# Dispatched experts: transposes at unit 0, a combine over three tiles, groups of 4, 9 and 3 sequences

## What is computed

```python
gate_probs = jax.nn.softmax(x @ Wg + bg, axis=-1)
_, top_idx = jax.lax.top_k(gate_probs, 2)
expert_mask = jax.nn.one_hot(top_idx, 8).sum(-2)
selected = gate_probs * expert_mask
selected = selected / (selected.sum(-1, keepdims=True) + 1e-08)
h = jax.nn.gelu(jnp.einsum('bsf,efh->bseh', x, W1) + b1)
expert_out = jnp.einsum('bseh,ehf->bsef', h, W2) + b2[None, None]
y = jnp.einsum('bsef,bse->bsf', expert_out, selected)
x = _layernorm(x + y, axis=-1)
```

## Time and profile before

| | us |
|---|---|
| median of 3 runs | 3257.44 |
| lowest, highest | 3252.2, 3268.81 |
| the profiled execution | 3267.32 |
| its span | 3265.6 |
| PE busy in it | 2630.8 (81%) |
| DVE busy | 2177.9 (67%) |
| ACT busy | 1415.1 (43%) |
| POOL busy | 1183.2 (36%) |
| stage of the change, from about 2692 to the end | 573 |

### The profile page before, as it was taken

The page is one execution under the profiler, slowest core; times in us unless marked ns, Lnnn a source line. Parts: engine busy times, 40 slices in busy tenths (PEclk is TensorE's granted clock), DMA queues, the critical chain, the costliest instruction groups (busy, mean ns, idle before and its releaser), DMA issues. The chain is left out here.

```text
span 3265.6 us, 51537 instructions
## 1 busy us (share of the span) xinstructions
PE 2630.8 (81%) x17479; PEld 2007.1 (61%) x17479; DVE 2177.9 (67%) x5628; ACT 1415.1 (43%) x2412; POOL 1183.2 (36%) x2298
## 2 busy tenths in 40 slices
PE   1445873999999999858888579999999975888972
PEld 1423662777777777546666467777777754666651
DVE  5733764777777777368888656676767636567684
ACT  0001320555555555412121136666666642776751
POOL 3210111344444434322222124444544444761165
PEclk9997995899999999879999879999999985999996
DMA  2144001222322213021110022212221207776662
GB/s 28 32 142 120 22 10 30 41 39 33 46 35 35 45 29 44 12 100 49 56 56 16 10 35 41 41 29 31 40 36 24 41 2 259 226 248 211 221 208 69
DMA packets 198657, 228.02 MB, mean 70 GB/s; under 512 B 48621, under 2 KB 148814, under 8 KB 190478
## 3 DMA queue, kind: packets, MB, share of 16 engines
q1 hardware_dynamic: 188302, 207.69, 26.4%
q0 software_dynamic: 8192, 16.79, 1.6%
q10 hardware_dynamic: 2048, 2.10, 0.2%
HBM read 132.55 MB, written 58.10 MB: 58 GB/s over the span
## 5 line engine op out<-in xcount | busy, mean ns | idle before, releaser
L1394 PE MATMUL banks<-Kb,Qb 96*128 96x128 f32 (+3 forms) x2048 | 600.0, 348 | 58.7 <-issue 27.1
L1406 PE MATMUL banks<-Qb,Kb 98*128 98x512 f32 (+3 forms) x2048 | 603.4, 356 | 4.8 <-ACT mla_prob L1297 1.0
L1101 DVE TENSOR_REDUCE mha_nm<-banks 128x1 f32<-128x384 f32 (+3 forms) x704 | 421.7, 639 | 189.3 <-PE banks L1398 175.9
L1101 DVE TENSOR_REDUCE mla_nm<-banks 128x1 f32<-128x384 f32 (+3 forms) x704 | 419.6, 637 | 157.2 <-PE banks L1398 143.8
L1297 ACT ACTIVATE mla_prob<-banks 128x512 f32<-128x512 f32 x640 | 376.6, 598 | 306.0 <-PE banks L1406 297.8
L1394 PEld LDWEIGHTS banks<-Kb,Qb 96*128 96x128 f32 x2048 | 364.2, 195 | 216.6 <-issue 157.4
L1297 ACT ACTIVATE mha_prob<-banks 128x512 f32<-128x512 f32 x640 | 376.0, 599 | 276.9 <-PE banks L1406 264.1
L1216 POOL TENSOR_SCALAR_AFFINE_SELECT mla_prob<-mla_prob 128x256 f32<-128x256 f32 (+1 forms) x640 | 239.1, 382 | 397.4 <-PE banks L1394 373.5
L1406 PEld LDWEIGHTS banks<-Qb,Kb 98*128 98x128 f32 x2048 | 335.3, 193 | 45.4 <-issue 6.0
L1216 POOL TENSOR_SCALAR_AFFINE_SELECT mha_prob<-mha_prob 128x256 f32<-128x256 f32 (+1 forms) x640 | 227.0, 363 | 357.3 <-PE banks L1394 331.2
L2174 DVE TENSOR_TENSOR moe_hl<-moe_h,moe_hh 128x512 fp32r<-128x512 f32 x212 | 146.6, 692 | 123.1 <-ACT moe_h L2278 118.2
(11 more groups left out here) (434 smaller groups left out, 5438.3 us busy)
## 6 DMA issues: line engine op xcount, KB each, us to landing
moe_wt<-expert_rows SPq DMA_DIRECT2D x53, 1024.0 KB, 5.1
conv_tz<-conv_kernel SPq DMA_DIRECT2D x16, 1024.0 KB, 6.8
moe_xg<-slots SPq DMA_DIRECT2D x53, 256.0 KB, 4.5
results<-moe_yt SPq DMA_DIRECT2D x53, 256.0 KB
Kb<-mla_kh SPq DMA_DIRECT2D x32, 256.0 KB, 5.0
Qb<-mla_qh SPq DMA_DIRECT2D x128, 64.0 KB
Kb<-mha_kh SPq DMA_DIRECT2D x32, 256.0 KB, 5.6
Qb<-mha_qh SPq DMA_DIRECT2D x128, 64.0 KB
```

The source lines that it names most:

```text
L1101: dve.tensor_reduce(nm[:, g % 2, h:h + heads, j], ps[:, bank1(g, k), 0:heads * w].rearrange("p (h k) -> p h k", h=heads), axis=AX.X, op=AL ...
L1394: one = pe.matmul(ps[:, bank, x * w:(x + 1) * w], Qb[0:MROW, u, g, h + x, j * P:(j + 1) * P], Kb[0:MROW, u, g, 0:w], start=(x == 0), stop= ...
L1406: last = pe.matmul(ps[:, S2 + k % 2, at:at + w], Kb[0:MROW + 2, u, grp, kb * P:(kb + 1) * P], Qb[0:MROW + 2, u, grp, h, kb * P:L], start=T ...
```

## The change

`TURN` becomes 0, 0, 1: the next tile's transposes follow unit 0, DVE's difference unit 1. `back` moves to unit 1, `keep` to unit 2. The combine is cut: at tile g DVE does the first half after unit 0 and the second half after unit 2, at tile g+1 the moments after unit 0, and at tile g+2 ACT normalises after unit 2 with four activations (scale and bias from a column each). POOL's root gets two more small operations, for the bias. The groups are 4, 9 and 3 sequences: 15, 25 and 13 tiles, still 53. The combines of group 0 stand at tiles 20, 22, 24, 25, of group 1 at 45, 47, 49, 50; the condition g + 2 < 53 puts the other five of group 1 with the three of group 2 into `LATE`, eight sequences. Experts 4 to 7 are prepared by DVE after `gates(1)` and by ACT after all sources and `power(1)`. The counts of group 0 come one sequence earlier.

```diff
-        GROUPS = ((0, 4), (4, 8), (12, 4))
+        GROUPS = ((0, 4), (4, 9), (13, 3))
-        TURN = dict(pe=1, act=1, dve=2)
-        EVAC, BACK, KEEP = 3, 0, 1
-        COUNT, POWER = GROUPS[0][1] + 4, GROUPS[0][1] + 4
+        TURN = dict(pe=0, act=0, dve=1)
+        EVAC, BACK, KEEP = 3, 1, 2
+        NORM = dict(dve=0, act=2)
+        COUNT, POWER = GROUPS[0][1] + 3, GROUPS[0][1] + 3
+        ORDER = [(q, j) for q, (_, n) in enumerate(GROUPS) for j in range(n)]
+        for i, (q, j) in enumerate(ORDER):
+            g = FIRST[q + 1] + 5 + (8 * j + 4) // 5 if q + 1 < len(GROUPS) else ALL
+            if g + 2 < ALL:
+                COMBINE[g] = i
+            else:
+                LATE.append(i)
...
+                def first_half(i):
                     dve.wait_ge(gathered[p], c.next(gathered[p], 2 * BLK * 16))
+                    if i >= 2:
+                        dve.wait_ge(out_ready, c.next(out_ready))
...
-                def norm(q, j):
-                    n, p = GROUPS[q][0] + j, j % 2
-                    dve.wait_ge(rstd_ready, c.next(rstd_ready))
...
-                    if q == 0:
+                    gates(q)
+                    if q == 1:
                         for e in range(RAWS, E1):
                             weights(e)
-                    gates(q)
...
                         if m == 0 and g in COMBINE:
-                            combine(*COMBINE[g])
-                        if m == EVAC and g in COMBINE:
-                            norm(*COMBINE[g])
+                            first_half(COMBINE[g])
+                        if m == 2 and g in COMBINE:
+                            second_half(COMBINE[g])
+                        if m == NORM["dve"] and g - 1 in COMBINE:
+                            moments(COMBINE[g - 1])
...
                 def root(p):
                     pool.wait_ge(mv_ready, c.next(mv_ready))
-                    pool_rstd(pool, c, pdone, mv[:, p, :, :], var[:, p, :], mhalf, rstd[:, p, :]).then_inc(rstd_ready, 1)
+                    pool.tensor_scalar(neg[:, p, :], mv[:, p, :, 0], -1.0, 0.0, ALU.mult, ALU.add)
+                    chain(pool, c, pdone, pool_rstd(pool, c, pdone, mv[:, p, :, :], var[:, p, :], mhalf, rstd[:, p, :]))
+                    pool.tensor_tensor(nmr[:, p, :], neg[:, p, :], rstd[:, p, :], ALU.mult).then_inc(rstd_ready, 1)
...
+                for i, (q, j) in enumerate(ORDER):
+                    early = j == 0 and i and i - 1 not in LATE
+                    if early:
+                        root((i - 1) % 2)
+                    if j == 0:
+                        pool.wait_ge(res_ready, c.next(res_ready))
+                    if i >= 2:
+                        pool.wait_ge(g_free, c.next(g_free))
...
+                    if i and not early:
+                        root((i - 1) % 2)
+                root((NB - 1) % 2)
...
+                power(1)
+                for e in range(RAWS, E1):
+                    weights(e)
+                power(2)
...
+                def norm(i):
+                    act.wait_ge(rstd_ready, c.next(rstd_ready))
+                    for b in range(BLK):
+                        last = act.activation(X[:, n, b, :], r[:, p, b, :], ACT.Identity,
+                                              bias=nmr[:, p, b:b + 1], scale=rstd[:, p, b:b + 1])
+                    last.then_inc(out_ready, 1)
```

More of the change, by code:

```diff
@@ L1998, in _ @@
                     load_x(g)
-                for g in range(ALL + 2):
+                for g in range(ALL + 3):
                     if g + XBUFS + 1 < ALL:
                         load_x(g + XBUFS + 1)
-                    if g >= 2:
+                    if 2 <= g < ALL + 2:
                         store_tile(g - 2)
@@ L2007, in _ @@
                         load_w(g + WBUFS - 1)
[L2008 to L2012, removed]
+                    if g - 3 in COMBINE:
+                        store_out(COMBINE[g - 3])
+                for i in LATE:
+                    store_out(i)
                 sp.wait_ge(stored, NB * 16)
@@ L2136, in combine, with moments @@
                     dve.sem_inc(g_free, 1)
+                def moments(i):
+                    p = i % 2
                     block_stats(dve, c, done, r[:, p, :, :], st, mv[:, p, :, :]).then_inc(mv_ready, 1)
-                def norm(q, j):
-                    n, p = GROUPS[q][0] + j, j % 2
-                    dve.wait_ge(rstd_ready, c.next(rstd_ready))
-                    for b in range(BLK):
-                        last = dve.tensor_scalar(X[:, n, b, :], r[:, p, b, :], mv[:, p, b, 0:1],
-                                                 rstd[:, p, b:b + 1], ALU.subtract, ALU.mult)
-                    link(last)
-                    dve.sem_inc(out_ready, 1)
                 def evacuate(g):
@@ L2187, in _ @@
                 keep(ALL - 1)
-                for i, (q, j) in enumerate(LATE):
-                    combine(q, j)
-                    if i:
-                        norm(*LATE[i - 1])
-                norm(*LATE[-1])
+                for i in LATE:
+                    first_half(i)
+                    second_half(i)
+                    moments(i)
             @block.gpsimd
@@ L2216, in _ @@
                                     X[:, first + j, b, :], None).then_inc(scattered[q], 16)
-                taken = 0
-                for q, (first, n) in enumerate(GROUPS):
-                    pool.wait_ge(res_ready, c.next(res_ready))
-                    for j in range(n):
-                        if taken >= 2:
-                            pool.wait_ge(g_free, c.next(g_free))
-                        taken += 1
-                        for b in range(BLK):
-                            for a in range(2):
-                                t = BLK * j + b
-                                pool.indirect_dma_start(
-                                    gb[:, j % 2, a, b, :], None, res_d[q],
-                                    bass.IndirectOffsetOnAxis(back_slot[:, q, a, t:t + 1], 0)).then_inc(gathered[j % 2], 16)
-                        if j:
-                            root((j - 1) % 2)
-                    root((n - 1) % 2)
+                for i, (q, j) in enumerate(ORDER):
[7 more added lines that the diff above has]
+                    for b in range(BLK):
+                        for a in range(2):
+                            t = BLK * j + b
+                            pool.indirect_dma_start(
+                                gb[:, i % 2, a, b, :], None, res_d[q],
+                                bass.IndirectOffsetOnAxis(back_slot[:, q, a, t:t + 1], 0)).then_inc(gathered[i % 2], 16)
+                    if i and not early:
+                        root((i - 1) % 2)
+                root((NB - 1) % 2)
             @block.scalar
@@ L2280, in _ @@
                             high_x((g + 1) % 2)
+                        if m == NORM["act"] and g - 2 in COMBINE:
+                            norm(COMBINE[g - 2])
+                for i in LATE:
+                    norm(i)
             @block.tensor
```

23 lines of the change are left out of this document (11 added, 12 removed).

## The result

The changed kernel takes 3246.2 us (median of 17 runs), the kernel before 3264.5 in as many runs beside it: a ratio of 0.9944, 95% interval 0.9931 to 0.9956. It is faster by 18.3 us, by little more than half of the 31.7 us of the sum. The 3246.2 us lie inside the range of 3211 to 3250, but outside the forecast's own 3215 to 3240; the kernel before was 7 us slower here than the 3257.4 from which the forecast counted.

The account below looks back on a forecast made before the run. PE bounds the loop, waiting each tile for DVE's difference of its input; scatter bounds before it, POOL after. 13.6 − 31.9 − 13.4 = −31.7 us, so 3257.4 becomes 3226 us, range 3211 to 3250.

Parts of the forecast that it names:

- Piece 1: Start of the stage to tile 0's first matmul: late expert weights delay it by 13.6 us, bounds +7.6 and +18.
- S: The start of tile 0, its first matmul: 2776.8 before, forecast at 2790.4.
- Rival A: At the start, tile 0's rows pass the weights or the weights' writes are quicker: 3213 to 3220 us; chance 0.12.
- The plain tile: In the loop, a tile without a combine takes 6.45 us instead of 7.39, as PE's wait goes.
- B: DVE or ACT lag in the loop, plain tiles take 6.9 us or combines stay dear: 3245 us; chance 0.20.
- C: PE waits at each unit's second product instead, tiles stay at 7.39 us: 3274 us, just slower; chance 0.07.
- D: Each normalisation reloads ACT's table, four times in piece 2: +10 to +20 us, 3241; chance 0.03.
- I count 4 us for group 0: Extra time of group 0's combines in the loop: 4 us, bounds 1 and 9.
- I cost it at nothing: In the loop, DMA share rises from 0.76 to 0.87; queues hold four tiles of weights ahead, so no cost.
- Piece 3: From group 1's first gather to the end, POOL's chain: 162 us instead of 175.4, −13.4.
- Rival E: Only half of 16 combines are spread and the tail dominates: piece 3 10 us longer, 3236 to 3246; chance 0.10.
- piece 2: From tile 0's first matmul to group 1's first gather: 281.6 us instead of 313.5, −31.9.

Follow-up runs that it names:

- space_fourth_third: The changed kernel with the combine of sequence 3 in tile 26 instead of 25; ratio 0.9932 to the kernel before.
- turn_only_again: The kernel before with only the next tile's transposes, DVE's difference, `back` and `keep` moved as in the change; ratio 0.9889 to the kernel before.
- no_wait_for_fourth: The changed kernel, with DVE waiting for sequence 3's gather only before the combine's second half (first half reads X); ratio 0.9934 to the kernel before.
- all_spaced: The kernel of all_mended_third_chip with combines two tiles apart in both groups; ratio 0.9844 to the kernel before.
- fifth_in_loop: The kernel of all_spaced with a fifth combine of group 1, sequence 8, in tile 51 of the loop; 3200.8 us, ratio 0.9799 to the kernel before.
- all_mended_third_chip: The changed kernel with experts 4 to 7's weights where they stood before, groups 4, 8, 4, and sequence 3's combine a tile later; ratio 0.9858 to the kernel before.
- the first eight runs: Two sets of four follow-up runs on two chips, changed kernel included; every kernel, that of before too, was 4 to 5% slower than otherwise.

## Why the prediction was right in its place and short in size

**Piece 1 was right.** Shifted by the 5.9 us, the forecast's times are 2753.5 for the end of the last weights (2753.1), 2764.2 and 2771.9 for the first and fifth load (2763.9, 2771.5), 2781.8 for the landing of tile 0's rows (2782.9) and 2784.5 for S (2785.65). Ring order, as the Trainium skill has it (DMA: Bandwidth & Descriptors, section Queues, rings and completion order, on HWDGE ordering), decided between +7.6 and +13.6: the trace agrees, with +14.7. Rival A is out.

**The plain tile was right**: 6.43 us for 6.45. Rivals B and C, a lag of DVE or ACT or a new wait at the second product, are out for plain tiles. That the time of 3246 is the one given for B is a coincidence: its tiles of 6.9 us are not there. D is out too: the stage has two loads of a table, as before, the later at 2755.54, ahead of the loop, and none for Identity; beside the blocked ones, no tile with a normalisation is more than 0.7 us over plain.

**The step that failed** lies in two sentences: "I count 4 us for group 0", and of the fuller DMA queues "I cost it at nothing". The combines cost 11.4 us, more than the upper bound of 9. The forecast had the fourth gather landing 2.7 us after DVE asks. DVE waited 5.83, and the difference is the landing: it took 4.7 us, where the tail, and the forecast's piece 3, have 1.5. space_fourth_third (gather ends 2958.26, DVE goes on 2963.39: 5.1 us) and turn_only_again (2890.21 and 2894.79: 4.6) show the same. And what hangs on that wait was not priced at all: DVE waits in order with the next tile's difference behind it, so 5.83 us of DVE are 7.00 of PE and then 4.0 us at half clock. The bounds weighed only DVE's work against its slack; no_wait_for_fourth shows that the place of the wait is the larger part. Without that one tile the combines cost 2.5 us, within the forecast's 4.

**Piece 3** was forecast with 162 and took 166.2. Its tail was right: six gathers with five roots took 70.0 us (3159.26 to 3229.27) for 70.3, the end behind them 11.6 for 11.7. The chain in the loop was 4.6 us too long (84.6 for 80). Its six gathers took 63.9 us, as taken (63.3), but POOL waited 2.8, 4.4 and 2.2 us for moments, 9.3 in all where 5 were counted; the longest stands behind a wait of DVE for a gather (2.85 us at 3126.69), the mechanism of group 0 again. Rival E, a tail that dominates, is out as priced: a root with its way back to the next gather took 2.1 us and a gather of the tail 9.8. But its neighbour is real: all_spaced and fifth_in_loop differ by one sequence in the tail and by 9.7 us.

**Where the gain went.** The move of the transposes brought 40.7 us in the stage. The rest of the change gave back 22.0: 15.7 at the start (99.1 for 83.4), 6.6 in piece 2, nothing in piece 3. The forecast had priced the start and the group's 12.9 us as costs, but not asked what the change would be without them; the late weights and the larger group alone cost 16.2 and 11.8 us, each undone by itself. By these two the combine in halves would have gained some 6 us (22.0 against 28.0), but no kernel has it alone and the edits do not simply add up. A direct comparison is all_mended_third_chip, which is turn_only_again with the combine cut, moved a tile later and spaced, and with earlier counts: its stage is 12.8 us shorter, 2.6 at the start and 14.4 in piece 2, with 4.1 lost in piece 3. fifth_in_loop is 20.4 us shorter than turn_only_again. So the cut combine pays, once no combine waits for its gather.

## What to carry to other kernels

When a loop gets faster, go over every fixed distance in it (a combine "four tiles after the group"): it was measured in tiles, while the gather behind it takes its microseconds, and its landing any time from 1.5 to 5.1 us. A landing read in the quiet tail is no price for one in the loop. Price a wait by what stands behind it in its engine's order, here the next tile's input and another engine's root, not by the work it starts. And price each edit of a change against leaving it out: one edit alone was worth twice the whole.

## What the runs showed of the hardware

- The landing of a gather, from the end of POOL's last instruction until the data are there, varies from 1.5 to 5.1 us. In the changed kernel the fourth of group 0 took 4.7 us, with a DMA share of 0.82 while it landed (row below); in the eight kernels that follow it in the table it took 4.3 to 5.1. It is not new with the change: the traces note when each gather's semaphore was raised, and in the kernel before the first gather of group 0 landed after 1.5 us, but the second after 4.7 (ended 2929.17, landed 2933.84, a DMA share of 0.88 between) and the third after 3.9. DVE asked for these later, so the forecast's rows did not show it. In the tail, with no loads of weights left, the last four gathers of every kernel of the table landed in 1.5 to 1.6 us. That the loads of weights beside it stretch the landing fits all of this, but no run varied them alone.

```profile
2952.70:2957.50 4.80, 1.51 (x7) 0.90 (x5) 0.07 (x1) 2.00 (x4) 0.00 (x0) 1.00 0.82 277
```

- POOL's gathers slow down where DVE works on a combine. In the window 2928.20 to 2940.60, with DVE busy 11.2 of 12.4 us, single gathers took up to 1.47 us and the eight together 12.4; in the next, with DVE busy 7.4 of 9.8, single ones took at most 1.08 and the eight together 9.8.

```profile
2928.20:2940.60 12.40, 12.21 (x62) 9.56 (x60) 11.19 (x29) 11.56 (x22) 10.23 (x8) 1.00 0.83 256
2942.90:2952.70 9.80, 9.55 (x48) 7.44 (x47) 7.42 (x16) 8.89 (x17) 7.66 (x8) 1.00 1.03 297
```

The Trainium skill (SBUF — State Buffer, section SBUF: two separate sides) describes a lock by which certain DVE operations keep GpSimd from writing descriptors. That the slow gathers coincide with DVE's work speaks for it; that this is the cause was not tested.
- In the first eight runs PE, ACT and DVE stood nearly still while POOL's scatters ran: one tile took 57 to 60 us, and in the three kernels that start earliest the next one 43 to 47. In the changed kernel PE was busy 10.7 of 58 us, at a DMA share of 0.13. The kernel with groups of 4, 8 and 4 ran once with the stop and once without on the same chip, so neither the chip nor the kernel alone decides it. The cause was not found.
